# Third layer of a graph network: source one-hots loaded by DMA transposes, target rows alone compared by VectorE and ScalarE

## The chip, the cores and the metric

The kernel runs on one core of one Trainium2 chip. The metric is the device time of one execution in microseconds (us), from the median of several runs. The engines are TensorE (PE in the profile, with its weight loads as PEld), VectorE (DVE), ScalarE (ACT), GpSimd (POOL) and SyncE (SP), which here only issues DMAs (its queue is SPq in the profile). The core has 16 DMA engines.

## The reference

Four layers of a graph network over N = 6250 nodes and E = 200000 edges (`src`, `dst`, sorted by `dst`), 64 features a node; after each layer the result is added to `x` and normalised. The change touches the third layer, in which every edge gets a coefficient from the dot product of its two ends:

```python
Wh = h @ W + b
Wr, Wc = Wh[row], Wh[col]                       # row = src, col = dst
dot = jnp.sum(Wr * Wc, axis=-1)
sim = dot / jnp.maximum(nr * nc, EPS)           # nr, nc: lengths of the two ends
base = adj_v * sc * no_diag
prop_pos = segment_sum((base * relu(sim))[:, None] * Wc, row, n_nodes)
prop_neg = segment_sum((base * -relu(-sim))[:, None] * Wc, row, n_nodes)
return scale * (coeff[0] * prop_pos + coeff[1] * prop_neg + coeff[2] * Wh)
```

## The kernel before, in words

The 6250 nodes are 49 blocks of 128 (`NB` = 49, `P` = 128). The edges are put into cells (j, i), j the block of the source and i the block of the target, with 128 slots a cell. A gather of node rows is a matmul with a one-hot: for each cell a 128x128 bf16 matrix that says which node of the block sits in which slot. 49 x 49 cells are worked through in 343 steps of seven cells (`G` = 7, `NQ` = 7, `NG` = 343): step n holds the cells of source block j = n // 7 and of target blocks 7 (n % 7) and the six behind it.

A first stage (100 to 1400 us of the trace) makes the slots and writes what the later layers read. Its one-hots with slots on the partitions and nodes along the columns go to DRAM as `OND` (targets) and `OSD` (sources); SP's queue stores them at lines 479 and 480, the latter in pieces of 128 bf16, 256 bytes. `ROWS` holds, for each cell, 128 source numbers and then 128 target numbers, as a row of 2 x 128 bf16.

The third layer (`pairs3_sp`, `pairs3_pe`, `pairs3_act`, `pairs3_dve`, `pairs3_pool`, lines 1089 to 1341) needs its gather one-hots the other way round: nodes on the partitions, slots along the columns. One step n goes through:

- SP, `columns` (line 1136): one DMA copies the step's seven cells of `ROWS` to all 128 partitions, into buffer `rw[n % 6]` (`NR` = 6), 1792 bf16 a partition. It waits until TensorE is done with step n - 6 (`r_got`). In SP's order the load of step n + 4 stands in step n. Behind it `hots` (line 1144) loads seven one-hots of `OSD` for the scatter.
- the comparison, `columns` of ACT and DVE: each element of `rw` becomes 1 where it equals the partition's number and 0 elsewhere. In two steps of three DVE does it in one `is_equal` (line 1278); in one step of three ACT does it with `Abs` and `Relu` (lines 1226, 1228). It too is done four steps ahead. Sources and targets of a cell are compared by the same instruction.
- PE, `ends`: 21 matmuls gather the target rows (line 1186, three bf16 parts of seven cells), and 21 the source rows (line 1193), both with `rw` as weights. The second half waits for `r_used` of step n - 2, that is for DVE.
- ACT, `ends` (line 1236) copies the target rows out of PSUM. DVE, `products` (lines 1286 to 1291) multiplies both and sums; after the seven steps of a block `coefficient` (lines 1297 to 1311) runs on DVE.
- the values to scatter, eight steps later, in three bf16 parts. Of the seven cells, `KA` = 3 are scaled by ACT (line 1245, an instruction a cell) and have their second part made by DVE (`remainder`, line 1315); the other four are GpSimd's (lines 1163 and 1168). GpSimd makes the third part of all seven (line 1173). PE scatters them with seven matmuls (line 1205).
- after each block a sum and an addition on DVE (lines 1331, 1333), after seven blocks a normalisation and the projection for the fourth layer.

No scheduler sets the order: each engine has a loop over n with the offsets written out, and semaphores tie the loops together. The fourth layer (lines 1344 to 1711) uses the same comparison on 896 bf16 a partition (lines 1596 and 1652).

```python
def columns(n):                       # DVE, line 1274
    if n % 3:
        r = n % NR
        dve.wait_ge(rows_ld[r].at, 16 * (n // NR + 1))
        hot_d.by(dve.tensor_scalar(rw[r], rw[r], iotap[:, 0:1], None, ALU.is_equal))
```

Of the kernel before, what the change touches and what calls it, by code (L numbers as in the profile page):

```python
# [14 lines left out]
P = 128  # L15
# [38 lines left out]
def gnn_kernel(nc, x, src, dst, eattr, ew, ew2, W1n, b1n, W1r, Wl1, bl1, W2n, b2n, W2r, Wl2, bl2,  # L54
               W2g, b2g, dcoef, cpar, spar, W3, watt, bias3, out):
    with ExitStack() as ctx:
# [1031 lines left out]

        G = GB
# [3 lines left out]
        rw = [part(2 * G * 64 * i, 2 * G * 64).bitcast(BF16) for i in range(NR)]  # L1093
# [9 lines left out]
        KA = 3  # L1103
        rows_ld = [sem(f"rows_ld{i}") for i in range(NR)]
        hot_a, hot_d = sem("ends_hot_act"), sem("ends_hot_dve")
# [3 lines left out]

        def on(s, o):  # L1110

            return Sem(s.at, o)
# [6 lines left out]
        def by_act(n):  # L1119

            return n // 3 + 1
# [9 lines left out]
        def pairs3_sp(sp):  # L1131
            def columns(n):
                r, c0 = n % NR, G * n
                if n >= NR:
                    sp.wait_ge(r_got.at, n - NR + 1)
                rows_ld[r].by(sp.dma_start(rw[r], ROWS[c0:c0 + G, :, :].rearrange("c f r -> (c f r)").partition_broadcast(P)), 16)

            def hots(m):

                if m >= 4:  # L1140
                    sp.wait_ge(os_ld[m % 4].at, 16 * (m // 4))
                if m >= NOS:
                    sp.wait_ge(spr.at, m - NOS + 1)
                os_ld[m % 4].by(sp.dma_start(osp[m % NOS].bitcast(BF16), OSD[m // NQ, :, GH * (m % NQ):GH * (m % NQ) + GH]), 16)

            sp.wait_ge(row_mm.at, 2 * NB)
            for n in range(4):
                columns(n)
            for n in range(NLAST):
                if n + 4 < NG:  # L1150
                    columns(n + 4)
                if 0 <= n - 3 < NG:
                    hots(n - 3)
# [21 lines left out]
        def pairs3_pe(pe):  # L1175
            def ends(n):
                r, h, j, i0 = n % NR, n % 2, n // NQ, G * (n % NQ)
                if n % 3:
                    pe.wait_ge(hot_d.at, n + 1 - by_act(n))
                else:  # L1180
                    pe.wait_ge(hot_a.at, by_act(n))
                if n >= 2:
                    pe.wait_ge(c_ev.at, n - 1)
                for k in range(G):
                    for s_ in range(3):
                        ins = pe.matmul(ps[h][:, 65 * k:65 * k + 65], rw[r][:, 2 * P * k + P:2 * P * k + 2 * P], Ws[:, i0 + k, s_, 0:65],  # L1186
                                        start=(s_ == 0), stop=(s_ == 2))
                c_got.by(ins)
                if n >= 2:
                    pe.wait_ge(r_used.at, n - 1)  # L1190
                for k in range(G):
                    for s_ in range(3):
                        ins = pe.matmul(ps[2 + h][:, 65 * k:65 * k + 65], rw[r][:, 2 * P * k:2 * P * k + P], Ws[:, j, s_, 0:65],  # L1193
                                        start=(s_ == 0), stop=(s_ == 2))
                r_got.by(ins)
# [25 lines left out]
        def pairs3_act(act):  # L1221
            def columns(n):
                if n % 3 == 0:
                    r = n % NR
                    act.wait_ge(rows_ld[r].at, 16 * (n // NR + 1))
                    ac.by(act.activation(rw[r], rw[r], ACT.Abs, bias=negp[:, 0:1]))
                    act.wait_ge(ac.at, ac.n)
                    hot_a.by(act.activation(rw[r], rw[r], ACT.Relu, bias=1.0, scale=-1.0))  # L1228
# [44 lines left out]
        def pairs3_dve(dve):  # L1273
            def columns(n):
                if n % 3:
                    r = n % NR
                    dve.wait_ge(rows_ld[r].at, 16 * (n // NR + 1))
                    hot_d.by(dve.tensor_scalar(rw[r], rw[r], iotap[:, 0:1], None, ALU.is_equal))  # L1278
# [109 lines left out]
        dlo_ld = [on(hot_st[i], 32 * len(range(i, NB * NH7, NHB))) for i in range(2)] \  # L1388
# [932 lines left out]
```

## Time and profile before

| | |
|---|---|
| median of 3 runs | 3968.42 us (3966.04 to 3969.57) |
| the profiled execution's own time | 3963.56 us |
| its span in the trace | 3961.8 us |
| mean granted TensorE clock | 0.907 of full speed |
| busy: PE, DVE, ACT, POOL | 78%, 83%, 57%, 35% of the span |

The median is 4.9 us above the profiled execution. Stages by the trace: head 0 to 100 us, slots and first layer to 1400, second layer to 1930, third to 2935, fourth to the end. In the rows, "mean ns of one" is an instruction's duration; two instructions of one engine can overlap a little, so that the sum of durations is slightly above busy time. "DMA share" and a queue's share are shares of the 16 DMA engines' time in the stretch.

### The profile page before, as it was taken

How to read it: one execution, taken by the hardware profiler on the slowest of the kernel's cores; microseconds unless marked ns; L12 is line 12 of the kernel's file. 1: busy time of each engine (PE TensorE's matmuls, PEld its weight loads, DVE VectorE, ACT ScalarE, POOL GpSimd, SP SyncE). 2: the span in 40 equal slices, each digit the busy share in tenths (PEclk: the TensorE clock that was granted, in tenths of full speed). 3: DMA queues.
4: the chain of work that ended last, by engine and by line, in shares of the span. 5: the costliest groups of instructions: out<-in, count | busy, mean ns of one | idle time of the engine just before them, and what ended most of it. 6: DMA issues, size and time to landing. Idle time of an engine off the chain costs nothing.

```text
span 3961.8 us, 125753 instructions
## 1 busy us (share of the span) xinstructions
PE 3079.3 (78%) x50473; PEld 2741.7 (69%) x50473; DVE 3283.6 (83%) x6987; ACT 2245.2 (57%) x5930; POOL 1372.6 (35%) x1644
## 2 busy tenths in 40 slices
PE   0288888888888859999777777777766888788786
PEld 0176667776677759899677777777755777777775
DVE  7599999999999933233699999999976989889897
ACT  5334444444444320000587888787855888888887
POOL 2000000000000000000287787787762555555554
PEclk9999999999999989999899998998986888878886
DMA  8156666666666679899677777777737888888884
GB/s 208 54 166 201 203 202 198 193 189 203 204 195 193 201 266 375 348 337 331 221 248 228 238 244 230 224 253 230 234 121 239 258 250 260 256 259 255 249 255 142
DMA packets 655940, 907.66 MB, mean 229 GB/s; under 512 B 363977, under 2 KB 587882, under 8 KB 636411
## 3 DMA queue, kind: packets, MB, share of 16 engines
q1 hardware_dynamic: 633240, 800.64, 63.1%
q10 hardware_dynamic: 19763, 94.38, 6.3%
q8 instruction: 406, 6.65, 0.7%
q0 software_dynamic: 2352, 4.52, 0.5%
q14 instruction: 179, 1.47, 0.1%
HBM read 651.96 MB, written 247.40 MB: 227 GB/s over the span
## 4 chain that ended last, share of the span: by engine, by line
DVE 35%; PE 34%; DMA 10%; ACT 9%; issue 8%; SPq 2%; POOL 1%; ACTq 1%; DVEq 0%; POOLq 0%
PE ps L639 7%; PE ps L979 7%; DVE U L769 4%; DMA U<-AD 4%; PE ps L664 3%; DVE U L1286 3%; DVE EDG L1315 3%; DMA T<-ROWS 3%; DMA A<-ROWS 2%; DVE U L1278 2%; PE ps L1193 2%; DVE U L1647 2%; ACT U L553 2%; DVE EDG L1652 2%; PE ps L1205 2%
## 5 line engine op out<-in xcount | busy, mean ns | idle before, releaser
L553 ACT ACTIVATE U<-ps 128x512 bf16<-128x512 f32 (+1 forms) x637 | 356.1, 576 | 493.0 <-PE ps L651 492.9
L1163 POOL TENSOR_TENSOR EDG<-U,edge 128x256 f32<-128x256 f32 x343 | 242.2, 706 | 848.8 <-DVE edge L1311 733.9
L1479 ACT ACTIVATE U<-U,T 128x65 f32<-128x65 f32 x1806 | 459.8, 339 | 108.7 <-PE ps L1567 96.9
L490 POOL DMA_INDIRECT U<-REC,nod x49 | 70.7, 1443 | 1190.3 <-PE ps L595 1068.0
L1193 PE MATMUL ps<-U 128*128 128x65 bf16 x7203 | 299.8, 198 | 214.0 <-DVE edge L1289 211.8
L979 PE MATMUL ps<-U 128*128 128x192 bf16 x4802 | 416.6, 247 | 37.6 <-DVE U L1056 21.3
L979 PEld LDWEIGHTS ps<-U 128*128 128x128 bf16 x4802 | 401.4, 98 | 46.3 <-DMA U<-AD 21.8
L792 DVE TENSOR_TENSOR EDG<-edge,EDG 128x896 bf16<-128x896 bf16 x686 | 411.0, 619 | 20.1 <-issue 11.9
L1193 PEld LDWEIGHTS ps<-U 128*128 128x128 bf16 x7203 | 261.1, 101 | 237.7 <-DVE edge L1289 234.9
L1505 POOL TENSOR_TENSOR U<-U 128x455 f32<-128x455 f32 x258 | 276.6, 1072 | 329.7 <-DVE U L1647 329.7
L664 PE MATMUL ps<-EDG,U 128*128 128x193 bf16 x2401 | 319.1, 256 | 76.8 <-ACT U L553 61.1
L639 PE MATMUL ps<-U 128*128 128x98 bf16 (+1 forms) x5292 | 356.6, 228 | 11.9 <-DVE U L769 11.9
L639 PEld LDWEIGHTS ps<-U 128*128 128x128 bf16 x5292 | 343.4, 101 | 23.8 <-DVE U L769 19.6
L1173 POOL TENSOR_TENSOR EDG<-EDG 128x448 f32<-128x448 f32 x343 | 331.2, 966 | 24.4 <-DVE EDG L1315 24.4
L1186 PE MATMUL ps<-U 128*128 128x65 bf16 x7203 | 299.0, 197 | 13.7 <-ACT U L1228 7.7
L651 PE MATMUL ps<-EDG 128*128 128x128 bf16 x2401 | 248.2, 223 | 64.3 <-DVE EDG L792 64.2
L769 DVE TENSOR_TENSOR U<-U 128x882 bf16<-128x882 bf16 x528 | 294.9, 612 | 0.0
L1186 PEld LDWEIGHTS ps<-U 128*128 128x128 bf16 x7203 | 281.1, 100 | 19.7 <-issue 11.5
L1245 ACT ACTIVATE EDG<-U,edge 128x64 f32<-128x64 f32 x1029 | 279.4, 338 | 18.4 <-DVE edge L1311 9.8
L664 PEld LDWEIGHTS ps<-EDG,U 128*128 128x128 bf16 x2401 | 188.4, 100 | 138.9 <-ACT U L553 128.8
L1061 DVE TENSOR_REDUCE A<-ps 128x64 f32<-128x192 f32 x98 | 34.3, 355 | 291.3 <-PE ps L979 291.1
L1236 ACT ACTIVATE U<-ps 128x455 f32<-128x455 f32 x343 | 184.9, 540 | 145.0 <-PE ps L1186 143.9
(305 smaller groups left out, 7585.7 us busy)
## 6 DMA issues: line engine op xcount, KB each, us to landing
U<-AD SPq DMA_DIRECT2D x98, 1568.0 KB, 8.5
U<-ROWS SPq DMA_DIRECT2D x343, 448.0 KB, 4.4
OND<-EDG SPq DMA_DIRECT2D x343, 224.0 KB
OSD<-EDG SPq DMA_DIRECT2D x343, 224.0 KB
AD<-U ACTq DMA_DIRECT2D x49, 1568.0 KB, 6.3
EDG<-ROWS SPq DMA_DIRECT2D x343, 224.0 KB, 5.0
U<-OND SPq DMA_DIRECT2D x303, 224.0 KB, 5.2
EDG<-OSD SPq DMA_DIRECT2D x189, 224.0 KB, 4.7
```

What stands on the lines that cost most here:

```text
L553: ev4.by(act.activation(prow[i % NPW][:, P * g:P * (g + m)], ps[4 + gg % 2][:, 0:P * m], ACT.Copy))
L639: ins = pe.matmul(ps[3][:, o:o + NB * (f1 - f0)], w_, FR[h][:, c, f0:f1, :, k], start=(h + c + k + f0 == 0), stop=(last and f0 == 0))
L664: ins = pe.matmul(ps[6][:, 0:XW], prow[i % NPW][:, P * j:P * j + P], Xs[:, j, :], start=(j == 0), stop=(j == NB - 1))
L769: ins = dve.tensor_tensor(FR[h][:, :, f, :, :], OH[j % 2][:, HC * h:HC * h + HC, :, :], bc(L_[j % NL][:, 2 + f, HC * h:HC * h + HC, :].uns ...
L792: ins = dve.tensor_tensor(o_[r].rearrange("p c (r k) -> p c r k", k=2), bc(r1v.unsqueeze(1), [P, 7, D, 2]), bc(sdb[i % 2][:, s, 7 * b:7 * ...
L979: ins = pe.matmul(ps[q][:, 0:192], arow[r][:, P * j:P * j + P], (XsB if p else XsA)[:, j, :, :].rearrange("p s f -> p (s f)"), start=(j == ...
L1173: low3.by(pool.tensor_tensor(V3[m % 4][:, 2, :, :], V3[m % 4][:, 1, :, :], S3[m % 4][:, 1, :, :], ALU.subtract))
L1186: ins = pe.matmul(ps[h][:, 65 * k:65 * k + 65], rw[r][:, 2 * P * k + P:2 * P * k + 2 * P], Ws[:, i0 + k, s_, 0:65], start=(s_ == 0), stop= ...
L1193: ins = pe.matmul(ps[2 + h][:, 65 * k:65 * k + 65], rw[r][:, 2 * P * k:2 * P * k + P], Ws[:, j, s_, 0:65], start=(s_ == 0), stop=(s_ == 2))
L1245: ins = act.activation(V3[m % 4][:, 0, k, :], Wc[:, j % 2, i0 + k, 0:D], ACT.Copy, scale=edge[:, 6 + j % 2, i0 + k:i0 + k + 1])
L1479: ins = act.activation(V4[k % NV][:, 0, c, :], H[d % 3][:, s, :], ACT.Copy, scale=a4[d % 2][:, s:s + 1])
L1505: look.by(pool.tensor_tensor(V4[k % NV][:, 2, :, :], V4[k % NV][:, 1, :, :], S4[k % NV][:, 1, :, :], ALU.subtract))
```

## The change

`rw` is laid out as two halves of seven cells, sources first. The source half is no longer compared: a DMA transpose reads seven one-hots of `OSD`, slots on the rows, and writes them with nodes on the partitions and slots along the columns. The target numbers come by a broadcast load of their own, 128 numbers (256 bytes) at a time out of every cell's row. Only the target half is compared, in even steps by DVE and in odd steps by ACT. `KA` goes from 3 to 4. The source gather on PE waits for the transpose. The semaphores that count the transposes are ones of the first stage, used again from the value they reached; the fourth layer's bases are shifted to fit.

```diff
-        rw = [part(2 * G * 64 * i, 2 * G * 64).bitcast(BF16) for i in range(NR)]
+        rw = [part(2 * G * 64 * i, 2 * G * 64).bitcast(BF16).rearrange("p (f k s) -> p f k s", f=2, s=P) for i in range(NR)]
-        KA = 3
+        KA = 4
+        turn_ld = [on(hot_st[i], 32 * len(range(i, NB * NH7, NHB))) for i in range(NHB)] \
+            + [on(rw_st[i], 32 * len(range(i, NB, 2))) for i in range(2)] + [on(ad_st[0], 16 * len(range(0, NB, NPW)))]
@@ by_act
-            return n // 3 + 1
+            return (n + 1) // 2
@@ pairs3_sp, columns
-                rows_ld[r].by(sp.dma_start(rw[r], ROWS[c0:c0 + G, :, :].rearrange("c f r -> (c f r)").partition_broadcast(P)), 16)
+                turn_ld[r].by(sp.dma_start_transpose(rw[r][:, 0, :, :], OSD[j, :, P * i0:P * (i0 + G)]), 16)
+                rows_ld[r].by(sp.dma_start(rw[r][:, 1, :, :], ROWS[G * n:G * n + G, 1, :].partition_broadcast(P)), 16)
@@ pairs3_pe, ends
-                if n % 3:
+                if n % 2:
+                    pe.wait_ge(hot_a.at, by_act(n))
+                else:
                     pe.wait_ge(hot_d.at, n + 1 - by_act(n))
-                else:
-                    pe.wait_ge(hot_a.at, by_act(n))
...
-                        ins = pe.matmul(ps[h][:, 65 * k:65 * k + 65], rw[r][:, 2 * P * k + P:2 * P * k + 2 * P], Ws[:, i0 + k, s_, 0:65],
+                        ins = pe.matmul(ps[h][:, 65 * k:65 * k + 65], rw[r][:, 1, k, :], Ws[:, i0 + k, s_, 0:65],
...
+                pe.wait_ge(turn_ld[r].at, turn_ld[r].o + 16 * (n // NR + 1))
...
-                        ins = pe.matmul(ps[2 + h][:, 65 * k:65 * k + 65], rw[r][:, 2 * P * k:2 * P * k + P], Ws[:, j, s_, 0:65],
+                        ins = pe.matmul(ps[2 + h][:, 65 * k:65 * k + 65], rw[r][:, 0, k, :], Ws[:, j, s_, 0:65],
@@ pairs3_act, columns
-                if n % 3 == 0:
+                if n % 2:
-                    ac.by(act.activation(rw[r], rw[r], ACT.Abs, bias=negp[:, 0:1]))
+                    ac.by(act.activation(rw[r][:, 1, :, :], rw[r][:, 1, :, :], ACT.Abs, bias=negp[:, 0:1]))
...
-                    hot_a.by(act.activation(rw[r], rw[r], ACT.Relu, bias=1.0, scale=-1.0))
+                    hot_a.by(act.activation(rw[r][:, 1, :, :], rw[r][:, 1, :, :], ACT.Relu, bias=1.0, scale=-1.0))
@@ pairs3_dve, columns
-                if n % 3:
+                if n % 2 == 0:
-                    hot_d.by(dve.tensor_scalar(rw[r], rw[r], iotap[:, 0:1], None, ALU.is_equal))
+                    hot_d.by(dve.tensor_scalar(rw[r][:, 1, :, :], rw[r][:, 1, :, :], iotap[:, 0:1], None, ALU.is_equal))
@@ fourth layer
-        dlo_ld = [on(hot_st[i], 32 * len(range(i, NB * NH7, NHB))) for i in range(2)] \
+        dlo_ld = [on(turn_ld[i], turn_ld[i].o + 16 * len(range(i, NG, NR))) for i in range(2)] \
```

## Rows read from the trace of the kernel before

**Rows 1.** Busy time by stretch of the span: third layer's steps, its end
```profile
core 0: us, PE busy (x) PEld busy (x) DVE busy (x) ACT busy (x) POOL busy (x), PEclk, DMA share, GB/s
...
1937.00:2928.00 991.00, 757.90 (x16793) 716.81 (x16790) 951.24 (x2089) 803.66 (x1667) 772.64 (x1003) 0.94 0.73 238
2928.00:2960.00 32.00, 16.86 (x88) 11.35 (x88) 13.72 (x32) 7.63 (x29) 19.54 (x27) 0.58 0.00 1
```
**Rows 2.** Who waited for whom in total, 1940 to 2900 us
```profile
engine line waited for: us in total, times, longest us
...
PE ps L1193 <- DVE edge L1289: 206.7, 134, 5.7
ACT U L1236 <- PE ps L1186: 140.1, 125, 4.0
...
ACT U L1226 <- DMA U<-ROWS: 1.2, 1, 1.2
```
**Rows 3.** The same for SP's queue, 1940 to 2900 us
```profile
SPq L1136 <- PE ps L1193: 661.6, 328, 7.7
```
**Rows 4.** Groups of instructions, 1940 to 2900 us: DVE's comparison and remainder, ACT's scaling
```profile
line engine op names shapes xcount | busy us, mean ns | idle before us <-releasers
...
L1245 ACT ACTIVATE EDG<-U,edge 128x64 f32<-128x64 f32 x972 | 264.0, 338 | 5.4 <-DVE edge L1311 5.3
...
L1315 DVE TENSOR_TENSOR EDG<-EDG 128x192 f32<-128x192 f32 x323 | 201.4, 623 | 18.8 <-ACT EDG L1245 18.0
...
L1278 DVE TENSOR_SCALAR U<-U,iotap 128x1792 bf16<-128x1792 bf16 x220 | 187.9, 854 | 0.0
```
**Rows 5.** Groups of instructions, 3000 to 3900 us (fourth layer): the comparison on 896 elements
```profile
L1652 DVE TENSOR_SCALAR EDG<-EDG,iotap 128x896 bf16<-128x896 bf16 x330 | 149.2, 452 | 0.1
...
L1596 DVE TENSOR_SCALAR T<-T,iotap 128x896 bf16<-128x896 bf16 x166 | 87.4, 526 | 35.2 <-DMA T<-ROWS 33.7
```
**Rows 6.** Single lines: durations min/median/max of DVE's and ACT's instructions
```profile
L1315 DVE TENSOR_TENSOR EDG<-EDG x343: 344/666/1143, 1954.2 to 2945.1; 128x192 f32<-128x192 f32 x172
...
L1236 ACT ACTIVATE U<-ps x343: 527/534/553, 1936.6 to 2923.6; 128x455 f32<-128x455 f32 x172
...
L1226 ACT ACTIVATE U<-U,negp x115: 1768/1777/1790, 1929.8 to 2917.7; 128x1792 bf16<-128x1792 bf16 x115
...
L1228 ACT ACTIVATE U<-U x115: 1696/1697/1699, 1931.6 to 2919.5; 128x1792 bf16<-128x1792 bf16 x115
```
**Rows 7.** DMA queues: SP's is q1; third layer, 1940 to 2900 us
```profile
q1 hardware_dynamic: 95123, 227.34, 72.2%
...
U<-ROWS SPq DMA_DIRECT2D x330, 448.0 KB, 4.4
EDG<-OSD SPq DMA_DIRECT2D x185, 224.0 KB, 4.6
```
**Rows 8.** DMA queues, fourth layer, 3000 to 3900 us
```profile
DMA packets 148649, 231.55 MB, mean 257 GB/s; under 512 B 21361, under 2 KB 148477, under 8 KB 148477
...
q1 hardware_dynamic: 148477, 229.23, 82.4%
```
**Rows 9.** DMA queues, first stage, 200 to 1350 us
```profile
DMA packets 349773, 225.84 MB, mean 196 GB/s; under 512 B 300087, under 2 KB 342811, under 8 KB 343867
...
q1 hardware_dynamic: 333951, 145.25, 44.3%
```
**Rows 10.** DMA queues, second layer, 1450 to 1900 us
```profile
q1 hardware_dynamic: 13731, 153.04, 90.2%
```
**Rows 11.** SP's DMA issues by line: time of one issue in ns
```profile
L480 SPq DMA_DIRECT2D OSD<-EDG x317: 422/437/1665, 211.3 to 1348.2; - x159
...
L1136 SPq DMA_DIRECT2D U<-ROWS x343: 319/320/1097, 1909.4 to 2908.6; - x172
...
L1144 SPq DMA_DIRECT2D EDG<-OSD x189: 354/378/1742, 1950.0 to 2909.0; - x189
```
**Rows 12.** Timeline, 2500 to 2512 us: TensorE's last use, the load, ACT's comparison
```profile
2502.84 0.98 PE L1193 MATMUL ps<-U 128*128 128x65 bf16 x21 [2.62 <-DVE edge L1289]
...
2503.84 0.32 SPq L1136 DMA_DIRECT2D U<-ROWS  x1
...
2511.48 1.78 ACT L1226 ACTIVATE U<-U,negp 128x1792 bf16<-128x1792 bf16 x1
```

More of the change, by code:

```diff
@@ L1086, in passes_dve, with on @@
             dve.wait_ge(ws_o.at, NGB)
+        def on(s, o):
+            return Sem(s.at, o)
         G = GB
@@ L1108, in gnn_kernel @@
         os_ld = [sem(f"os_ld{i}") for i in range(4)]
-        def on(s, o):
-            return Sem(s.at, o)
         rem3, low3, rem3p = on(hid, NB), on(relu, NB), on(outp, NB)
@@ L1132, in columns @@
             def columns(n):
-                r, c0 = n % NR, G * n
+                r, j, i0 = n % NR, n // NQ, G * (n % NQ)
                 if n >= NR:
                     sp.wait_ge(r_got.at, n - NR + 1)
-                rows_ld[r].by(sp.dma_start(rw[r], ROWS[c0:c0 + G, :, :].rearrange("c f r -> (c f r)").partition_broadcast(P)), 16)
+                turn_ld[r].by(sp.dma_start_transpose(rw[r][:, 0, :, :], OSD[j, :, P * i0:P * (i0 + G)]), 16)
+                rows_ld[r].by(sp.dma_start(rw[r][:, 1, :, :], ROWS[G * n:G * n + G, 1, :].partition_broadcast(P)), 16)
             def hots(m):
```

## The prediction

> **What bounds the kernel now.** I read the busy times by stretch first. In the third layer's steady part, 1937 to 2928 us, DVE is busy 951 of 991 us, ACT 804, PE 758, POOL 773, and the DMA engines 0.73 of the time [rows 1]. 343 steps in 991 us are 2.89 us a step. DVE at 96% is the bound; nobody else has less than 19% to spare. The waits say the same: PE's source gather waits 206.7 us for DVE's last use of a PSUM bank, ACT waits 140.1 us for PE, which stands behind DVE, and SP's queue waits 661.6 us for PE to free a row buffer [rows 2, 3]. For the row load itself there is one wait of 1.2 us in the whole layer [rows 2]. So whatever is taken off DVE shortens the layer, until something else reaches its own sum.
>
> **DVE's part.** Removed: 228 comparisons of 1792 elements at 0.854 us [rows 4], 194.7 us (343 steps less ACT's 115 [rows 6]). Added: 172 comparisons of 896 elements. The same instruction stands in the fourth layer at 0.452 us and, just behind load waits, 0.526 us [rows 5]; I take 0.452, the one without waits: 77.7 us (with the other 90.5). `KA` from 3 to 4 makes the remainder 256 wide instead of 192. Alone it takes 0.344 us, on average 0.623 [rows 4, 6]; the difference is contention with GpSimd, whose two instructions shrink by a quarter in turn. Scaled with the width, the 64 more columns cost between 0.344/3 = 0.11 and nothing (all of it fixed cost, or given back by the lighter GpSimd); I take 0.07, nearer the upper end, since 192 columns of a 0.344 us instruction can't all be fixed cost: 343 x 0.07 = 24 us. Net: -194.7 + 77.7 + 24 = **-93 us**, from 951 to 858 us busy. With the same 40 us of idle time the steps would take 898 us, 2.62 us each.
>
> **ACT's part.** Removed: 115 pairs of 1.777 + 1.697 us [rows 6], 399.5 us. Added: 171 pairs of 896 elements. Between 455 elements (0.534) and 1792 (1.737 as the mean of the two) [rows 6] the slope is 0.90 ns an element, so 0.93 us for 896: 342 x 0.93 = 318 us. A fourth scaling costs 264.0/972 = 0.27 us of busy time [rows 4], 93 us. ACT goes from 804 to 816 us: 91% of 898, close behind DVE but not ahead of it. In an odd step it works 0.53 + 4 x 0.27 + 1.9 = 3.5 us and in an even one 1.6; the comparisons are four steps ahead, which evens this out. I cost it at nothing as long as the step stays above 816/343 = 2.38 us. GpSimd loses a quarter of two of its three instructions, and PE's 49 matmuls a step are the same.
>
> **The DMA engines' part.** This is what is left, and here the change adds work. I count in time of one DMA engine. In the fourth layer q1 moved 127,116 packets of 1792 bytes (148,477 less 21,361 small ones) in 0.824 x 900 x 16 = 11,866 us, which, less the small ones, is 0.091 us a packet [rows 8]. In the first stage it carried 317 target stores of 128 such packets and 317 source stores of 896 packets of 256 bytes, in 0.443 x 1150 x 16 = 8151 us [rows 9]; without the former (3692 us) that leaves 0.0157 us a small packet (the two prices are solved for together). Now a step of the third layer uses 0.722 x 960 x 16 / 330 = 33.6 us [rows 7], of which the one-hot load for the scatter has 128 x 0.091 = 11.6.
> After: the scatter's one-hots 11.6; the target numbers, 128 partitions x 7 cells in pieces of 256 bytes, 896 x 0.0157 = 14.1 (the whole row load of twice the bytes took 22.0); and the transpose T, which no row shows. It moves 128 x 896 bf16. Its lower bound is a plain load of the same bytes, 11.6 us of engine time, 0.73 us on all 16. Its upper bound is that each 256-byte piece is paid for twice, 28.2 (1.76 us), once read and once turned. I take 14.1 (0.88 us), what 896 pieces cost, because a piece of a one-hot is 128 columns of a row, as in the stores: near the lower end, since the cost of a piece has in its row both a read and a write. Sum: 11.6 + 14.1 + 14.1 = 39.8 us, or 2.49 us on 16 engines. The best that this queue held over a long stretch is 0.902 [rows 10]; I take that as full: 2.49 / 0.902 = **2.76 us a step**.
> The Trainium skill has two rules that differ here. "DMA: Bandwidth & Descriptors", section "Latency and other measured facts", gives 261 GB/s for a DMA transpose whose middle dimension is not contiguous, an estimate of 0.88 us for these 229 KB, at which the sum stands as above. "Advanced Engine Details and Errata", section "X-Bar Transpose (TRN2)", says that transposes run as fast as other DMAs, at 350 to 400 GB/s, an estimate of 0.57 to 0.66 us, at which DVE would stay the bound (the first rival). No trace of before shows a transpose.
>
> **SP's queue.** Its issues take 0.32 us for the rows and 0.38 for the one-hots [rows 11]. The row load in seven pieces is like the store in seven pieces, 0.44 [rows 11]. The transpose's own issue lies between 0.32 (any load) and 4.4 us, the time to landing [rows 7], if the queue were held until it is done. I take 1.2 us, between the two and nearer the short one, since every issue in the trace is far shorter than its landing: 2.0 us a step with the gaps, within 2.76. Behind it in the queue stand the row load and the one-hot load of the same step; ACT and DVE wait for the former, PE for the latter. Cover: the load goes out at 2503.84 us, as PE's last matmul ends, and ACT compares it at 2511.48, 7.6 us later, 4.4 of it to landing [rows 7, 12]. So 3.2 us are free, at 2.76 us steps 2.9; 1.2 are used up by the transpose ahead. PE needs the transpose itself only in its own step, later still.
>
> **Ends.** The first four loads go out at 1909 us, 20 us before use [rows 6, 11]. In the tail of 32 us [rows 1], ACT and GpSimd pass values to each other; one more scaling there is about 0.1 us x 8 steps, nothing. The fourth layer's counts move only.
>
> **Sum.** DVE's sum gives 2.62, the DMA engines' 2.76; the larger sets the step. 343 x 2.76 = 947 against 991: -44 us. The profiled execution took 3963.6 us, so 3920; the median of the runs is 4.9 above it, so 3924 us. A measurement of this kernel tells 0.2%, 8 us, from no change.
>
> **Rivals.**
> 1. The transposes are cheap, DVE stays the bound. It decides when T is under 2.62 x 0.902 x 16 - 25.7 = 12.1 us of engine time (0.76 us), and the result is 3968 - 93 = 3875. For it: the lower bound lies there, and the share of time that packets took at 0.73 has waiting in it that closes up under load. Against: small pieces cost 21% more per byte than large ones (0.0157 us for 256 bytes, 0.091 for 1792). Chance 0.27.
> 2. The transposes cost the DMA engines more. From T = 2.89 x 0.902 x 16 - 25.7 = 16.0 us (1.00 us on all 16) on, the step is longer than before: the queue fills, rows land late, ACT waits for them and everyone for ACT. A quarter above that point, T = 20, gives 45.7/16/0.902 = 3.17 us, +95 us: 4063; at the upper bound 3.73 us, +289: 4257. For it: T needs only 14% over my value. Against: the range from 1.00 to 1.76 us asks for a cost per piece that no row shows. Chance 0.18.
> 3. The issue of a transpose holds SP's queue. It decides from 2.89 - 0.44 - 0.38 - 0.1 = 1.97 us of hold. If it is half of the landing time, 2.2 us, the step is 3.12 us, +79 us: 4047. For it: the three issues of a step are in one queue, and the transpose goes first. Against: no issue now takes a tenth of its landing. Chance 0.14.
> Between, with T at about 1.00 us, nothing moves (0.08). My forecast has 0.33.
>
> **How the numbers follow.** Faster is the forecast and rival 1, 0.60; same 0.08; slower rivals 2 and 3, 0.32. The range goes from somewhat under rival 1 (DVE's contention less than taken, another 10 us) to just over the prices of 2 and 3: 3865 to 4070. Left out are a twentieth below and the dearer part of rival 2, some 0.12, above. The forecast's own range is 3885 to 3955.
>
> **What the profile after would show.** DVE's comparison x172 at about 0.45 us, ACT's two x171 at 0.93, the remainder at about 0.7. DVE's share of the layer down from 96% to about 91, the DMA share up from 0.73 to about 0.9, and landing times over 5 us. ACT or DVE waits for DMA U<-ROWS or PE for DMA U<-OSD, tens of us where there was 1.2. Wrong if DVE is still at 96% (rival 1), if q1's share is high at steps of over 2.9 us (rival 2), or if the transpose's issue is over 2 us with the DMA share low (rival 3). All other stages should be unchanged; if they are not, the reasoning has missed something.

## The result, and the profile after

The changed kernel takes 4085.93 us (median of 4 runs, 4078.37 to 4096.35) against 3967.45 us; the ratio is 1.03, with a 95% interval of 1.0277 to 1.0323. It is 118 us slower. The forecast was 3924 us, 43 us faster, and the range ended at 4070.

The third layer accounts for it: it takes 136 us longer, and in the profiled execution it begins 13 us earlier, which is no more than its beginning moves from run to run (1924 to 1948 us in the runs that keep the first stage as it is). DVE's first product (line 1286 before, 1291 after) starts step by step from 1937.2 to 2927.9 us before, 2.90 us a step, and after:

```profile
L1291 DVE TENSOR_TENSOR U<-ps,U x343: 608/617/625, 1924.4 to 3050.7; 128x448 f32<-128x448 f32 x172
```

That is 1126.3 us over 342 steps, 3.29 us each, 0.40 us more. The busy times by stretch, to set beside [rows 1]:

```profile
core 0: us, PE busy (x) PEld busy (x) DVE busy (x) ACT busy (x) POOL busy (x), PEclk, DMA share, GB/s
1937.00:3046.00 1109.00, 778.55 (x16482) 724.95 (x16483) 795.15 (x2005) 809.58 (x2089) 644.09 (x996) 0.92 1.16 210
```

No engine is a bound any more: DVE is at 72% where it was at 96%, ACT at 73%, PE at 70%. The bytes moved fell from 238 to 210 GB/s although the DMA share reads 1.16. A share over 1 means that packets are recorded as overlapping in time, so it is no measure of how full an engine is here; which packets these are is told under what stays open.

Who waited for whom, 1940 to 3000 us, beside [rows 2]:

```profile
DVE U L1283 <- DMA U<-ROWS: 265.3, 114, 4.2
ACT U L1231 <- DMA U<-ROWS: 255.1, 149, 3.9
PE ps L1198 <- DVE edge L1294: 250.7, 151, 6.5
```

The same for SP's own queue, beside [rows 3]:

```profile
SPq L1139 <- PE ps L1198: 97.8, 120, 2.6
```

Before, the row load had caused one wait of 1.2 us; now both engines that compare stand 255 to 265 us for it. SP's queue, which had waited 661.6 us for PE to free a buffer, waits 97.8. There is no line in which PE waits for the transpose itself. The trace has the landing of only 57 of the 343 transposes, so I looked at the other side: PE's weight loads for the source gather pause for more than 0.2 us 163 times, and each of these pauses ends within 0.1 us of DVE's instruction, so none is a wait for a transpose. It is the load *behind* the transpose that is late. What SP's queue does in that time, on the timeline from 2499 us (start, duration, engine and line):

```profile
2499.10 1.31 SPq L1139 DMA_TRANSPOSE U<-OSD  x1
2500.46 1.05 SPq L1140 DMA_DIRECT2D U<-ROWS  x1
2501.61 2.34 SPq L1148 DMA_DIRECT2D EDG<-OSD  x1
2503.99 1.23 SPq L1139 DMA_TRANSPOSE U<-OSD  x1
2505.26 0.58 SPq L1140 DMA_DIRECT2D U<-ROWS  x1
2505.94 0.51 SPq L1148 DMA_DIRECT2D EDG<-OSD  x1
2506.49 1.24 SPq L1139 DMA_TRANSPOSE U<-OSD  x1
2507.77 0.58 SPq L1140 DMA_DIRECT2D U<-ROWS  x1
2508.45 1.34 SPq L1148 DMA_DIRECT2D U<-OSD  x1
2509.84 2.43 SPq L1139 DMA_TRANSPOSE U<-OSD  x1
```

One issue follows the other without a pause. A transpose takes the queue 1.23 us at the least and 1.24 at the median, the row load behind it takes 0.58 where the whole row load took 0.32, and now and then an issue is stretched to 2.3 or 2.4 us. Added up over 2000 to 2850 us of this timeline the three lines take 1.52 + 0.67 + 0.93 = 3.12 us of 3.3 a step. Of this, 0.30 us are waits for PE to free a buffer, which lie inside the records of the transposes; the issues themselves are 2.82.

The DMA queue and the loads over 1940 to 3000 us, beside [rows 7]:

```profile
q1 hardware_dynamic: 634472, 220.13, 115.2%
...
U<-ROWS SPq DMA_DIRECT2D x320, 224.0 KB, 4.9
EDG<-OSD SPq DMA_DIRECT2D x180, 224.0 KB, 5.1
U<-OSD SPq DMA_DIRECT2D x140, 224.0 KB, 5.1
U<-OSD SPq DMA_TRANSPOSE x320, 5.1
```

The last figure is the median of those transposes whose landing is recorded.

And what the change was to win on DVE, from the groups of the same stretch, beside [rows 4]:

```profile
L1320 DVE TENSOR_TENSOR EDG<-EDG 128x256 f32<-128x256 f32 x318 | 165.9, 522 | 8.5 <-ACT EDG L1250 7.4
...
L1283 DVE TENSOR_SCALAR U<-U,iotap 128x896 bf16<-128x896 bf16 x160 | 82.8, 518 | 265.5 <-DMA U<-ROWS 265.3
```

The DVE side did come. The remainder, a third wider, takes 0.52 us where it took 0.62. That is the pace of this kernel, in which GpSimd is busy 58% of 2000 to 2850 us against 79% before; at the pace of a kernel that DVE bounds it is 0.62 again, as no_turn will show.

### The profile page after: what moved, and what is told of

It is laid out like the page before. It is cut to its first block, busy times and chain, and to the rows that moved or that the text cites. A ratio compares the mean times of both kernels' runs of the same rounds, so it can differ in the third digit from the quotient of the medians.

```text
span 4076.6 us, 126836 instructions
## 1 busy us (share of the span) xinstructions
PE 3097.1 (76%) x50473; PEld 2752.4 (68%) x50473; DVE 3142.1 (77%) x6931; ACT 2261.8 (55%) x6385; POOL 1247.3 (31%) x1644
## 3 DMA queue, kind: packets, MB, share of 16 engines
q14 instruction: 186, 1.52, 0.1%
## 4 chain that ended last, share of the span: by engine, by line
PE 31%; DVE 28%; DMA 16%; SPq 9%; ACT 8%; issue 6%; ACTq 1%; POOL 1%; DVEq 0%; POOLq 0%
DMA U<-ROWS 8%; PE ps L979 7%; PE ps L639 7%; DVE U L769 4%; SPq L1139 4%; DMA U<-AD 3%; PE ps L664 3%; PE ps L1198 3%; DMA A<-ROWS 2%; DMA T<-ROWS 2%; SPq L1148 2%; DVE U L1652 2%; DVE EDG L1657 2%; ACT U L553 2%; DVE EDG L792 2%
## 5 line engine op out<-in xcount | busy, mean ns | idle before, releaser
L1198 PE MATMUL ps<-U 128*128 128x65 bf16 x7203 | 309.9, 201 | 262.3 <-DVE edge L1294 262.0
L1167 POOL TENSOR_TENSOR EDG<-U,edge 128x192 f32<-128x192 f32 x343 | 182.7, 533 | 978.0 <-DVE edge L1316 729.3
L1250 ACT ACTIVATE EDG<-U,edge 128x64 f32<-128x64 f32 x1372 | 361.4, 338 | 9.3 <-PE ps L1210 5.7
L1190 PE MATMUL ps<-U 128*128 128x65 bf16 x7203 | 306.5, 199 | 59.9 <-ACT U L1241 52.3
L1231 ACT ACTIVATE U<-U,negp 128x896 bf16<-128x896 bf16 x171 | 178.0, 1041 | 270.9 <-DMA U<-ROWS 270.8
L1283 DVE TENSOR_SCALAR U<-U,iotap 128x896 bf16<-128x896 bf16 x172 | 88.6, 516 | 281.6 <-DMA U<-ROWS 281.3
```

The source lines that it names most:

```text
L1190: ins = pe.matmul(ps[h][:, 65 * k:65 * k + 65], rw[r][:, 1, k, :], Ws[:, i0 + k, s_, 0:65], start=(s_ == 0), stop=(s_ == 2))
L1198: ins = pe.matmul(ps[2 + h][:, 65 * k:65 * k + 65], rw[r][:, 0, k, :], Ws[:, j, s_, 0:65], start=(s_ == 0), stop=(s_ == 2))
L1250: ins = act.activation(V3[m % 4][:, 0, k, :], Wc[:, j % 2, i0 + k, 0:D], ACT.Copy, scale=edge[:, 6 + j % 2, i0 + k:i0 + k + 1])
```

## The experiments

The theories, as the expectations name them: E, the packets of the transposes fill the DMA engines; H, the issue of a transpose holds SP's queue; P, the pieces of 256 bytes of the row load are what costs; L, the row load lands late behind the transpose; Q, one queue for three loads lets the engines run dry. Each run is the changed kernel with one edit, unless said otherwise; its diff shows the lines that matter, with `...` where others are left out. "Step" is DVE's first product from first to last start, divided by 342. The kernel before measured between 3965.6 and 3974.7 us beside them.

| | time, us | ratio to before, 95% interval | step, us |
|---|---|---|---|
| before | | | 2.90 |
| changed kernel | 4085.9 | 1.0300 (1.0277 to 1.0323) | 3.29 |
| no_turn | 3888.2 | 0.9786 (0.9762 to 0.9810) | 2.69 |
| tiny_turn | 3907.1 | 0.9837 (0.9811 to 0.9863) | 2.75 |
| plain_load | 3884.8 | 0.9788 (0.9761 to 0.9815) | 2.71 |
| pieces_load | 4004.7 | 1.0095 (1.0070 to 1.0120) | 3.03 |
| rows_first | 4037.8 | 1.0180 (1.0163 to 1.0197) | 3.11 |
| whole_rows | 3986.9 | 1.0059 (1.0041 to 1.0076) | 2.84 |
| double_turn | 4490.3 | 1.1322 (1.1290 to 1.1355) | 4.48 |
| extra_tiny | 4367.5 | 1.0996 (1.0979 to 1.1012) | 4.09 |
| extra_plain | 4304.6 | 1.0843 (1.0823 to 1.0863) | 3.91 |
| hots_by_act | 4056.8 | 1.0211 (1.0191 to 1.0232) | 3.16 |
| mixed | 3955.8 | 0.9973 (0.9957 to 0.9989) | 2.77 |
| mixed_old_rows | 3937.8 | 0.9907 (0.9892 to 0.9923) | 2.79 |
| mixed_by_third | 3964.0 | 0.9981 (0.9962 to 1.0000) | 2.88 |
| mixed_fixed | 3927.9 | 0.9892 (0.9876 to 0.9907) | 2.80 |
| mixed_first | 3933.7 | 0.9901 (0.9887 to 0.9915) | 2.79 |

### What takes the transpose's place

**no_turn.** The transpose and PE's wait for it are gone, and the source gather reads the target half, so it computes other values:

```diff
-                turn_ld[r].by(sp.dma_start_transpose(rw[r][:, 0, :, :], OSD[j, :, P * i0:P * (i0 + G)]), 16)
...
-                pe.wait_ge(turn_ld[r].at, turn_ld[r].o + 16 * (n // NR + 1))
...
-                        ins = pe.matmul(ps[2 + h][:, 65 * k:65 * k + 65], rw[r][:, 0, k, :], Ws[:, j, s_, 0:65],
+                        ins = pe.matmul(ps[2 + h][:, 65 * k:65 * k + 65], rw[r][:, 1, k, :], Ws[:, j, s_, 0:65],
...
```

> The changed kernel without its 343 transposes: the source half is not loaded, and TensorE's source gather reads the target half. Changed: 3.29 us a step. Theory E (the transposes' packets fill the DMA engines): the step falls to what DVE and ACT need, 2.6 us, 343 x 0.69 = -235 us, about 3850; the row load waits vanish. Theory H (the issue of a transpose holds SP's queue): the same fall, this run alone can't tell it from E. Theory P (the row load in 256-byte pieces is what costs): no more than half of that fall, 3950 to 4000, with row waits of over 100 us left.

3888 us, 2.69 us a step. This is what DVE's relief is worth when nothing is paid for it: DVE is busy 804 of 850 us again, and neither DVE nor ACT waits for a load. 3850 us had been expected, and the prediction had 2.62 us a step. DVE's two changed instructions, 2000 to 2850 us:

```profile
L1318 DVE TENSOR_TENSOR EDG<-EDG 128x256 f32<-128x256 f32 x312 | 192.2, 616 | 27.7 <-ACT EDG L1248 27.5
...
L1281 DVE TENSOR_SCALAR U<-U,iotap 128x896 bf16<-128x896 bf16 x156 | 106.5, 683 | 0.0
```

**tiny_turn.** The same instruction with 1/56 of the data; the source gather reads the target half here too:

```diff
-                turn_ld[r].by(sp.dma_start_transpose(rw[r][:, 0, :, :], OSD[j, :, P * i0:P * (i0 + G)]), 16)
+                turn_ld[r].by(sp.dma_start_transpose(rw[r][:, 0, 0, 0:16], OSD[j, 0:16, P * i0:P * i0 + P]), 16)
...
```

> A transpose of 16 x 128 elements in the place of each of 128 x 896: the same instruction and the same count of issues in SP's queue, but 1/56 of the data; the source gather reads the target half. Theory E: the step falls to 2.6 us as without transposes (about 3850 to 3870), with SP's issue still about 1.2 us. Theory H: it stays near 3.29 us or falls little (over 4000), and SP's queue is busy all the time.

2.75 us, 19 us over no_turn, between the two forecasts and much nearer to E's. Its issues are 1.09 us at the least. So the hold of one transpose a step is nearly covered as long as nothing else fills the queue; alone it does not make the changed kernel slow. ACT and DVE wait 48.5 and 34.9 us for rows between 2000 and 2850 us, which shows it is close.

**plain_load** and **pieces_load.** The transpose's 229 KB, not turned, in runs of 1792 bytes or in pieces of 256; neither turns the one-hots, so the source gather's values are others:

```diff
-                turn_ld[r].by(sp.dma_start_transpose(rw[r][:, 0, :, :], OSD[j, :, P * i0:P * (i0 + G)]), 16)
+                turn_ld[r].by(sp.dma_start(rw[r][:, 0, :, :].rearrange("p k s -> p (k s)"), OSD[j, :, P * i0:P * (i0 + G)]), 16)
```
```diff
-                turn_ld[r].by(sp.dma_start_transpose(rw[r][:, 0, :, :], OSD[j, :, P * i0:P * (i0 + G)]), 16)
+                turn_ld[r].by(sp.dma_start(rw[r][:, 0, :, :], OSD[i0:i0 + G, :, P * j:P * j + P].rearrange("i p r -> p i r")), 16)
```

> In the place of each transpose a plain load of the same seven one-hots, not turned, 128 packets of 1792 bytes. Theory E with the turning as its cost: DMA sum 11.6 + 14.1 + 11.6 = 37.3 us of engine time a step, 2.58 us at 0.902, so 2.62 to 2.7 us a step, 3855 to 3890. If the bytes themselves were the cost (any third load of 229 KB too much): over 3950.

> In the place of each transpose a plain load of the same bytes in 896 pieces of 256 bytes, 14.1 us of engine time by the prediction: 39.8 us in all, 2.76 us a step, about 3920. Theory E with the turning as its cost: near that, 3880 to 3950. Theory P (256-byte reads are dearer than the stores from which they were priced): over 4000, close to the changed kernel, and the DMA queue's packets of 256 bytes take well over 0.0157 us each.

The bytes are free (2.71 us, 3885 us), the pieces are not: 3.03 us, 120 us more, and already slower than before, by 0.7 to 1.2%. Two loads of a step in pieces of 256 bytes, the target numbers and this one, are enough to lose the whole gain. Its queue, 2000 to 2850 us:

```profile
q1 hardware_dynamic: 548288, 191.84, 95.3%
```

0.953 x 850 x 16 / 279 steps = 46.5 us of engine time; less the one-hots (11.6) that is 34.9 us for 1792 pieces, 0.0195 us each. In no_turn it was 0.639 x 850 x 16 / 310 = 28.0, less 11.6 = 16.4 us for 896, 0.0183 each:

```profile
q1 hardware_dynamic: 328235, 143.46, 63.9%
```

The prediction had priced them by the first stage's stores, 0.0157. The mean times of the single packets in the traces put this more finely: a 256-byte packet took 16.4 ns as a store of the first stage, 17.9 ns in no_turn and 18.6 in pieces_load, and a 1792-byte packet of the one-hots 81 ns in the third layer before, 90 in no_turn and 99 in pieces_load. So a load in pieces is 16.7 us in pieces_load, not 17.4, and the one-hots are 12.7 there, not 11.6: every packet takes longer in a fuller queue.

### The order, and the rows in one run

**rows_first.** The row load is issued ahead of the transpose.

> The changed kernel with the two loads of a step swapped: target numbers first, transpose behind them. Theory E (the DMA engines are full): the order changes nothing that lasts, 3.2 to 3.3 us a step, within 15 us of the changed kernel's 4086; row waits may turn into waits of TensorE for the transpose. Theory L (the row load lands late because it stands behind the transpose, and the six-buffer loop sets the pace): the row load goes out 1.2 us earlier, the step falls by about 1.24/4 = 0.3 us, about 3985.

4038 us: 48 us back, half of what theory L asked for and more than theory E allowed. SP now waits 16.0 us of 850 for PE, against 79.8 in the changed kernel, so its queue is the one thing that never pauses.

**whole_rows.** `ROWS` is stored as (49, 2, 49 x 128), so that seven target rows are one run:

```diff
-        ROWS = dram("ROWS", (NC, 2, P), BF16)
+        ROWS = dram("ROWS", (NB, 2, NB * P), BF16)
...
-                rows_ld[r].by(sp.dma_start(rw[r][:, 1, :, :], ROWS[G * n:G * n + G, 1, :].partition_broadcast(P)), 16)
+                rows_ld[r].by(sp.dma_start(rw[r][:, 1, :, :].rearrange("p k s -> p (k s)"), ROWS[j, 1, P * i0:P * (i0 + G)].partition_broadcast(P)), 16)
```

> The changed kernel with ROWS laid out so that the target numbers of seven cells are one run of 1792 bytes: 128 packets instead of 896, transposes kept. From the first four runs, at 0.96 of the 16 engines: 11.6 (one-hots) + 17.4 (rows in pieces) + T = 50.6 in the changed kernel, so T = 21.6 us of engine time. Theory E: 11.6 + 11.6 + 21.6 = 44.8 us, 2.92 us a step, -130 us against the changed kernel, about 3957 and no difference from the kernel before. If the transpose alone held the pace (theory H in combination with its start in the engines): no more than 30 us gained.

The step falls from 3.29 to 2.84 us, more than the 0.37 expected: with transposes kept, the pieces of the row load alone are worth 0.45 us a step. The kernel gains 99 us by the medians (the profiled execution, 3958.5 us, lies 28 under its median), not 155, because the new layout costs the first stage: ACT's row store (line 534) takes its queue 0.787 us instead of 0.268 and the next one 0.507 instead of 0.330, 49 times, and the third layer begins at 1956 us.

### Data or instruction

**double_turn, extra_tiny, extra_plain.** Behind each transpose goes a second one, a transpose of 16 x 128, or a plain load of the same 229 KB, each into six scatter buffers that nobody reads, which leaves ten of sixteen for the scatter; PE's source gather waits for both. The lines of extra_tiny:

```diff
-        NOS = len(osp)
+        NOS = len(osp) - 6
...
+                turn_ld[r].by(sp.dma_start_transpose(osp[10 + r].bitcast(BF16)[:, 0:16], OSD[j, 0:16, P * i0:P * i0 + P]), 16)
...
```

> The changed kernel with every transpose issued twice, the second into six of the sixteen scatter buffers (ten are left), which nobody reads. Theory E: T = 21.6 us of engine time more, 72.2 us in all at 0.96, 4.7 us a step, 4086 + 343 x 1.41 = 4570. Theory H: SP's queue gets 1.24 us more of issue, of which it has about 0.75 us in hand for waits on a full queue: at most 3.8 us a step, 4260.

> The changed kernel with a second transpose behind each, of 16 x 128 elements, into scatter buffers that nobody reads (ten of sixteen are left): one more issue and hold of SP's queue, 1.1 us by tiny_turn, and almost no data. A full second transpose cost 1.19 us a step (double_turn). Theory E (the transpose's data on the DMA engines): a small part of that, 0.3 us a step at most, under 4190. Theory H (each transpose holds the queue and what stands behind it starts late, whatever its size): 0.9 to 1.2 us a step, 4390 to 4500.

> The changed kernel with one more plain load of the 229 KB of each step, not turned, 128 packets of 1792 bytes, into the same unread buffers. Theory E: 11.6 us more on engines that are full, 0.73 to 0.76 us a step, about 4340. Theory H: its issue, 0.5 us a step, of which waits on a full queue give some back: under 4260.

A whole second transpose costs 1.19 us a step, one with hardly any data 0.80, and a plain load of all the data 0.61. For extra_tiny theory H had 4390 for the least, theory E 4190 for the most: at 4368 it is much nearer to H. For double_turn, at 4490, both missed: H had 4260 for the most, E 4570. Two thirds of what a second transpose costs in this queue does not depend on its size. The smaller number of scatter buffers costs nothing that shows: in double_turn, extra_tiny and extra_plain SP's only waits are those of line 1139. The granted clock, on the other hand, was 0.79, 0.82 and 0.83 in this stretch where the changed kernel had 0.92, and how much of the added time is TensorE's was not separated. In extra_tiny, 2000 to 2850 us, the engines are far from full and everyone waits all the same:

```profile
q1 hardware_dynamic: 418030, 142.54, 80.2%
```

```profile
DVE U L1284 <- DMA U<-ROWS: 356.1, 97, 5.9
ACT U L1232 <- DMA U<-ROWS: 335.3, 101, 5.1
```

SP's issues there, from the single lines (min/median/max, ns):

```profile
L1139 SPq DMA_TRANSPOSE U<-OSD x343: 1250/1252/3116, 1915.2 to 3324.3; - x172
L1140 SPq DMA_TRANSPOSE EDG<-OSD x343: 1114/1225/2048, 1916.7 to 3325.6; - x172
L1141 SPq DMA_DIRECT2D U<-ROWS x343: 366/581/1246, 1917.9 to 3326.8; - x172
```

extra_plain (4305) lies between the theories' figures of 4340 and 4260. Its 0.61 us a step is close both to its issue of 0.58 us and to 11.6 us on full engines (0.73), so it decides nothing.

**hots_by_act.** The other half of the question: the engines' work is the same, but the scatter's one-hots leave SP's queue.

```diff
-                os_ld[m % 4].by(sp.dma_start(osp[m % NOS].bitcast(BF16), OSD[m // NQ, :, GH * (m % NQ):GH * (m % NQ) + GH]), 16)
...
+                os_ld[m % 4].by(act.dma_start(osp[m % NOS].bitcast(BF16), OSD[m // NQ, :, GH * (m % NQ):GH * (m % NQ) + GH]), 16)
```

> The changed kernel with the one-hot loads for the scatter issued by ACT's queue instead of SP's; the DMA engines move the same bytes in the same packets. SP's queue is left with the transpose and the row load, about 0.6 us a step less to issue. Theory E (the engines' packets are the limit, 3.29 us a step): no change, 4070 to 4100. Theory Q (a single queue is the limit: what stands behind a transpose is issued late, and the engines run dry meanwhile): the step falls towards ACT's new sum of (816 + 343 x 0.4)/343 = 2.8 us, 3925 to 3990.

4057 us, 29 us better and no more: 13 us below theory E's figures and 67 above theory Q's. SP now waits 277.0 us of 850 for PE. Its transposes take 2.28 us at the median instead of 1.24:

```profile
L1139 SPq DMA_TRANSPOSE U<-OSD x343: 1227/2279/4701, 1912.1 to 3003.3; - x172
```

Most of that growth is no hold. Between 2000 and 2850 us 168 of the 267 transposes have the end of a wait for PE inside their record, 257 us together; the other 99 take 1.68 us at the median. So with less to issue, SP's queue has time to spare, and the step is still 3.16 us: something on the side of the engines binds as well. Theory Q alone is refuted by this run, theory E alone by extra_tiny.

### Versions that would beat both

**mixed** turns in odd steps only; even steps load whole rows and DVE compares them, `KA` is 3, and `ROWS` has the layout of whole_rows. **mixed_old_rows** is the same with the old layout of `ROWS`; it put the whole rows down in another order than PE reads them, so its even steps compute with other one-hots. **mixed_fixed** reads them at the right offsets, **mixed_first** also issues the rows of an odd step first. **mixed_by_third** leaves ACT's comparison as before and turns in three quarters of DVE's steps, with the rows issued first; its whole rows are out of order as in mixed_old_rows. SP's loads in mixed_old_rows and mixed_fixed:

```diff
...
+                if n % 2:
+                    turn_ld[r].by(sp.dma_start_transpose(rw[r][:, 0, :, :], OSD[j, :, P * i0:P * (i0 + G)]), 16)
+                    rows_ld[r].by(sp.dma_start(rw[r][:, 1, :, :], ROWS[G * n:G * n + G, 1, :].partition_broadcast(P)), 16)
+                else:
+                    rows_ld[r].by(sp.dma_start(rw[r].rearrange("p f k s -> p (f k s)"), ROWS[G * n:G * n + G, :, :].rearrange("c f r -> (c f r)").partition_broadcast(P)), 16)
...
```

> Transposes in odd steps only (ACT compares the target half there); in even steps whole rows, compared by DVE, as before; rows in the layout of whole_rows, KA = 3. DMA engines: (44.8 + 34.9)/2 = 39.9 us, 2.60 us a step at 0.96. DVE: 172 comparisons of 1792 at 0.854 instead of 228, -48 us, 2.75 us a step, about 3920, faster than both kernels. Theory H gives 1.24 us of hold every other step, also covered. If the queue's order makes waits anyway: 3940 to 3970.

> mixed with the old layout of ROWS. mixed took 2.77 us a step in the third layer (before: 2.90) but began it some 29 us later, since its row stores take ACT's queue 0.69 us longer, 49 times. Theory: DVE is the bound at 2.75, DMA engines (11.6 + 17.4 + 19 + 33.6)/2 = 40.8 us, 2.66 us a step: the 29 us come back and the 44 us stay, about 3922. If small row pieces stall odd steps: 3940 to 3960.

> ACT compares whole rows in one step of three, as before; of DVE's 228 steps three quarters (171) have transposes and compare 896 elements, 57 whole rows; KA = 3, row load ahead of the transpose, old layout of ROWS. DVE: 171 x 0.452 + 57 x 0.854 = 126 us instead of 195, -69 us, 2.70 us a step; DMA engines 2.66. About 3900, the fastest so far, if DVE stays the bound; 3920 to 3945 if DMA waits take a part.

> mixed_old_rows with the whole rows of the even steps in the order in which ROWS has them, seven times (128 sources, 128 targets), which TensorE reads at the fitting offsets; the same instructions and bytes: the same time, 3938 within 8 us, faster than both kernels.

> mixed_fixed with the row load of an odd step ahead of its transpose. In mixed_old_rows ACT waited 47 us of 850 for rows; in the changed kernel the same swap gave 48 us back. Where DVE is the bound (97% busy in the layer) it should give 0 to 20 us: 3918 to 3938.

mixed_fixed is the best, 3927.9 us, 1.1% under the kernel before, and mixed_first can't be told from it. In 2000 to 2850 us DVE is the bound again, at 820 of 850:

```profile
2000.00:2850.00 850.00, 671.88 (x14861) 639.51 (x14858) 819.56 (x1815) 661.73 (x1596) 689.60 (x903) 0.93 1.12 247
```

mixed was forecast at about 3920 us and took 3956; its 2.77 us a step was forecast at 2.75, and its late start of 29 us came from the row stores, as whole_rows shows, and went with the old layout. mixed_old_rows took 3938 where 3922 was forecast, at 2.79 us a step. With DVE as the bound the order of the loads is worth nothing (mixed_first). mixed_by_third was a miss: it was to be the fastest at 2.70 and took 2.88. Its DVE is busy 797 of 850 us, 94%, and ACT had kept its pairs of 3.5 us; whether these or the uneven places of the transposes cost it was not separated.

## Why the prediction was wrong

**What bounds the kernel now: right.** DVE at 96% was the bound. Taking its work away without a price gives 2.69 us a step (no_turn).

**DVE's part: right, 10 us too good.** Where DVE is the bound (no_turn) the comparison took 0.683 us, not 0.452, and the remainder 0.616, not 0.69. Over the layer the first is 40 us more than forecast and the second 25 less. The 0.07 us for the 64 more columns is what they cost alone (0.409 us at the least against 0.344), but on average they came free, which fits GpSimd's lighter work giving it back, one of the two ends that the text had named. In the changed kernel itself, where DVE waits for loads, the two took 0.518 and 0.522. The step reached 2.69 and not 2.62 because DVE was busy 868 us of 1937 to 2860, not 858, and idle 55, not 40.

**ACT's part: right.** 1.04 + 0.95 us a pair against 0.93 each, and 810 us busy against 816. It never was the bound.

**The DMA engines' part: the step that failed first.** "896 x 0.0157 = 14.1" for the target numbers took its price from stores to DRAM; as a load the same pieces came to 16.0 to 16.4 us in no_turn and 16.7 to 17.4 in pieces_load. For T the text took the same 14.1. With plain loads in pieces in both places (pieces_load) the sum is 46.5 us and not 39.8, 5 of the 7 us from the pieces and the rest from the one-hots, and the step is 3.03 us, not 2.76. This alone is worth 0.27 us a step and turns the sign: no transpose is needed to lose. The forecast had said of the range above 1.00 us that it "asks for a cost per piece that no row shows", and 16.7 us is 1.04.

The transpose itself costs more again. The records of the changed kernel come to 1.149 x 850 x 16 / 256 = 61.0 us a step. Less the one-hots (12.2), the rows at 16.7 and the smallest packets (0.6), T is 31.6 us: an estimate of 17.5 us in packets that take about 20 ns, a little more than a plain piece, and 14.1 us in a few packets that stay open for long (see what stays open). Together with the queue's holds this is the way from 3.03 to 3.29 us.

**"I take that as full", of 0.902: off the other way.** pieces_load holds 0.953.

**SP's queue: the size was right, the use of it was not.** The hold was taken as 1.2 us and is 1.24. But the text made two sums, 2.76 us for the engines and 2.0 for the queue, and let the larger set the step, as if neither lengthened the other. The runs show that they add up in part: a transpose of almost nothing costs 0.06 us a step where it is the only one (tiny_turn) and 0.80 behind a whole one (extra_tiny), and taking the one-hots out of the queue gives back 29 us. The row load behind a transpose also takes 0.58 us of issue, not 0.44. Together that is 1.24 + 0.58 + 0.51 = 2.33 us of smallest or usual issues a step and 0.8 us on top, 0.3 of it waits for PE and the rest stretched issues. Stretched issues alone prove no hold by the transposes: in pieces_load, without any transpose, the three lines take 2.84 of 3.05 us a step. The 3.2 us that the text had counted as free ahead of ACT's comparison were used up, as ACT's and DVE's waits of 255 and 265 us show.

**The rivals.** Rival 2 (the transposes cost the engines more, 4063) and rival 3 (the issue holds SP's queue, 4047) had 0.18 and 0.14. Both happened at once, and each was priced without the other, which is why the time lies beyond the range's end, where 0.12 of the chance had been left. Of the signs named in advance, rival 2's came, a high share of q1 at steps over 2.9 us, though the share is swollen by the open packets; rival 3's, an issue over 2 us with the share low, did not. Rival 3's turning point, 1.97 us of hold, was reached neither by the instruction (1.24) nor on average (1.52, waits for PE included): it left the other issues at their sizes of before.

**The rule of bandwidth.** With the Trainium skill the prediction weighed 261 GB/s for a transpose ("DMA: Bandwidth & Descriptors", section "Latency and other measured facts") against 350 to 400 ("Advanced Engine Details and Errata", section "X-Bar Transpose (TRN2)"). They differ less than it said: the first page gives the 261 for a middle dimension that is not contiguous and 350 to 400 for the contiguous case. Neither describes what was paid here: as a second transpose (double_turn less extra_tiny) the data of 229 KB cost 1.19 - 0.80 = 0.39 us more than almost nothing, less than the 0.57 us of the faster rule, and the instruction itself 0.80. A rule in bandwidth alone can't give a time for a transpose of this size in a queue with others. No run times a transpose by itself.

**What stays open.** What, beside the holds, makes a transpose dearer than pieces. Counting the bytes of the packets that start in each quarter microsecond between 2000 and 2850 us, almost nothing (under 30 GB/s) moves for 96 us in the changed kernel, 78 in extra_tiny and 122 in mixed_fixed, but for 3 in pieces_load and 16 in plain_load. Such time is no mark of transposes by itself: it is 80 us in the kernel before and 88 in no_turn, where SP's queue waits for PE most of the time and about one load is under way in it. In the changed kernel three plain loads are issued and not landed in that time, on average, so it is not for want of work. Half-microsecond slices of 2500 to 2520 us, in the changed kernel:

```profile
DMA  6679997059999998899900089999999999999994
GB/s 142 139 229 316 242 124 36 25 113 283 228 266 279 291 231 187 210 292 266 142 0 2 9 188 283 255 254 289 290 260 227 270 321 191 224 184 257 293 271 53
```

and in pieces_load:

```profile
DMA  9999999999968899999998868899866899998996
GB/s 290 235 251 292 254 222 212 256 299 281 188 151 171 246 326 290 241 260 218 300 287 191 210 154 136 267 313 280 182 128 147 270 320 300 278 245 222 300 271 151
```

The gap at 2510 us is not one with the engines at rest. While it lasts, 21 packets of 256 bytes stand open that began between 2509.1 and 2509.9 and take 1.8 to 2.6 us each, where the median packet takes 18 ns. Between 2000 and 2850 us the changed kernel has 2594 packets of 256 bytes that are open over 0.5 us, in 149 stretches of 1.4 us at the median. For 94 of the 96 us one of them is open; all their stretches together are 211 us, in which 79 GB/s move, against 253 in the rest. These packets are also what takes the share over 1. In pieces_load, whose pieces have the same size, and in tiny_turn none takes over 0.13 us. So the stretches come with whole transposes. The trace does not say to which transfer a packet belongs; by their size and their absence elsewhere I take them for a transpose's own, which would make this a stall inside the transfer with loads waiting behind it. What makes it, and how the 0.26 us between 3.03 and 3.29 divide between it and the hold of SP's queue, no run shows.

## What to carry to other kernels

A load that gets its own order of bytes (pieces of 256 instead of runs of 1792 or 3584 bytes) has to be priced by a *load* of such pieces, and where none is in the trace its bound belongs in the range at full weight; here it was worth more than the feature it served. Work that moves from a compute engine to a DMA queue is to be summed over that queue as an engine of its own, and its holds do not simply hide behind the transfers: here they hid when there was one tiny transpose a step and not behind a whole one. A conversion by halves (every second step) gained 43 us, about half of the 81 that a full one is worth where nothing is paid for it (no_turn), and left DVE the bound. A record of an issue that also waits for a semaphore has to be split into wait and hold before its length is read as a price.

## What the runs showed of the hardware that was not expected

- The issue of a DMA transpose takes 1.09 us with 16 x 128 elements (tiny_turn) and 1.23 to 1.25 us with 128 x 896; a plain load issued right behind one takes 0.58 us, where the same load ahead of it takes 0.43 at the median (rows_first).
- A few packets of some of the 128 x 896 transposes stay open for 0.5 to 2.7 us, and little else moves meanwhile: 79 GB/s against 253 in the changed kernel.
- Behind a transpose of 128 x 896 in a busy queue, a second one of 16 x 128 costs 0.80 us a step and one of 128 x 896 1.19.
- 896 pieces of 256 bytes read from DRAM take the engines 16 to 17 us of their time, the same bytes in 128 runs 11.6 to 12.7.
- DVE's remainder with 256 columns takes 0.409 us at the least, 0.522 on average where GpSimd is busy 58% of the time (changed kernel) and 0.616 where it is busy 73% (no_turn); with 192 columns it took 0.623 at 79% (before).
